# Second pair of a routed mixture-of-experts layer sorted by expert, first pair sorted one stage sooner

## What is computed

```
x = layernorm(h)
attn_out = softmax(q k^T / 4) v                      # 16 heads, all 512 keys, q k v = x W_qkv + b
gate = softmax(x W_gate + b_gate)                    # 8 experts
combine = the two largest gates of each token, zero for the other six experts
moe_out = sum over e of combine[e] * (x W_experts[e] + b_experts[e])
h = h + attn_out + moe_out
```

## Time and profile before

| what | us |
|---|---|
| median of 3 runs | 599.95 (599.64 to 600.82) |
| profiled execution, its span | 600.7 |
| TensorE busy | 539.3 (90%) |
| VectorE busy | 424.7 (71%) |
| ScalarE busy | 285.8 (48%) |
| GpSimd busy | 188.1 (31%) |
| stages 0 to 7, from each one's first score product | 51.0, 53.0, 53.1, 69.5, 60.7, 96.3, 85.2, 79.8 |

### The profile page before, as it was taken

How to read it: one execution, slowest core, us unless ns; L and a number is a source line. 1 busy time by engine, 2 the same in 40 slices (tenths; PEclk the granted TensorE clock), 3 DMA queues, 4 the chain that set the end, 5 groups by cost and what they waited for, 6 DMA issues and landing times.

```text
span 600.7 us, 9520 instructions
## 1 busy us (share of the span) xinstructions
PE 539.3 (90%) x3209; PEld 283.9 (47%) x3209; DVE 424.7 (71%) x941; ACT 285.8 (48%) x558; POOL 188.1 (31%) x257
## 2 busy tenths in 40 slices
PE   3968998989899899998888899989999999999996
PEld 2435554654565335334533456444545555544442
DVE  6757766667877895887678877656876566678841
ACT  0314454536544563676354343525565455444444
POOL 6444746223422600211243233202233331043201
PEclk9978999999999999999997899999999999999999
DMA  6364534222332343353235132403259667232311
GB/s 194 103 199 129 159 95 156 68 74 81 116 89 67 111 113 100 94 158 102 71 94 154 55 108 86 124 18 113 67 174 267 191 201 238 70 104 72 108 54 35
DMA packets 45151, 69.23 MB, mean 115 GB/s; under 512 B 9208, under 2 KB 38320, under 8 KB 42416
## 3 DMA queue, kind: packets, MB, share of 16 engines
q1 hardware_dynamic: 40672, 55.64, 31.5%
q0 software_dynamic: 4224, 12.59, 6.8%
q10 hardware_dynamic: 208, 0.40, 0.2%
HBM read 45.25 MB, written 23.07 MB: 114 GB/s over the span
## 4 chain that ended last, share of the span: by engine, by line
PE 67%; DVE 18%; issue 7%; DMA 3%; ACT 3%; POOL 1%; ACTq 0%; SPq 0%; DVEq 0%
PE OB L1593 12%; PE R L1473 10%; PE R L1368 9%; PE SC L1543 8%; PE ST L1566 7%; DVE neg_max L1048 5%; PE R L1383 4%; PE R L1459 4%; PE SC L1548 3%; PE ST L1572 2%; PE R L1419 2%; PE R L1487 2%; DVE neg_max L1056 2%; DMA QS<-shiftT 2%; PE SC L1553 2%
## 5 line engine op out<-in xcount | busy, mean ns | idle before, releaser
L1048 DVE TENSOR_REDUCE neg_max<-SC 128x1 f32<-128x512 f32 x256 | 170.8, 687 | 78.1 <-PE SC L1543 74.9
L909 ACT ACTIVATE prob<-ST 128x512 f32<-128x512 f32 x256 | 136.7, 598 | 123.9 <-PE ST L1566 118.7
L1593 PE MATMUL OB<-prob,VS 128*32 128x512 f32 (+2 forms) x1024 | 107.2, 491 | 0.1
L1543 PE MATMUL SC<-KS,QS 96*128 96x512 bf16 x256 | 97.6, 389 | 8.6 <-DVE neg_max L1048 6.6
L912 ACT ACTIVATE prob<-ST 128x512 f32<-128x512 f32 (+1 forms) x128 | 68.0, 543 | 68.2 <-PE ST L1572 67.9
L745 POOL TENSOR_SCALAR_AFFINE_SELECT prob<-prob 128x512 f32<-128x512 f32 x64 | 40.9, 639 | 131.1 <-ACT prob L912 131.0
L1566 PE MATMUL ST<-QS,KS 98*128 98x512 bf16 x256 | 77.5, 380 | 1.9 <-ACT prob L909 1.9
L1056 DVE TENSOR_REDUCE neg_max<-SC 128x2 f32<-128x512 f32 x64 | 44.1, 688 | 22.0 <-PE SC L1553 21.6
L1053 DVE TENSOR_REDUCE neg_max<-SC 128x1 f32<-128x128 f32 (+1 forms) x128 | 39.6, 351 | 25.8 <-PE SC L1553 25.5
L1548 PE MATMUL SC<-KS,QS 96*128 96x256 bf16 (+1 forms) x256 | 48.0, 270 | 6.2 <-DVE neg_max L1053 2.7
L1543 PEld LDWEIGHTS SC<-KS,QS 96*128 96x128 bf16 x256 | 24.8, 97 | 55.1 <-DVE neg_max L1048 35.9
(11 more groups left out here) (156 smaller groups left out, 765.1 us busy)
## 6 DMA issues: line engine op xcount, KB each, us to landing
scratch<-parts SPq DMA_DIRECT2D x96, 128.0 KB
QS<-scratch SPq DMA_DIRECT2D x42, 256.0 KB, 3.3
KS<-scratch SPq DMA_DIRECT2D x42, 256.0 KB, 3.9
x_sorted<-ys SPq DMA_DIRECT2D x24, 128.0 KB, 3.2
xs<-x_sorted SPq DMA_DIRECT2D x12, 256.0 KB
y_sorted<-ys SPq DMA_DIRECT2D x12, 256.0 KB
QS<-scratch SPq DMA_DIRECT2D x12, 128.0 KB, 2.6
w_exp<-in_L_ffn_W_experts SPq DMA_DIRECT2D x6, 256.0 KB, 3.3
```

The costliest lines, as they stand in the source:

```text
L909: act.activation(prob[:, u % 2, e, :], src[:, :], ACT.Exp, scale=SCALE).then_inc(s_prob, 1)
L1048: dve.tensor_reduce(own_max[:, i, head:head + 1], bank[:, :], AX.X, ALU.max, negate=True).then_inc(s_max, 1)
L1543: pe.matmul(bank[:, :], Q[0:SHIFT_ROW, head, i * P:(i + 1) * P], K[0:SHIFT_ROW, head, :], start=True, stop=True).then_inc(s_sc_ps, 1)
L1593: mm = pe.matmul(OB[VW * i:VW * (i + 1), columns], VS[s % 3][:, kt, v:v + VW], p_of, start=(kt == 0), stop=(kt == NT - 1), skip_group_chec ...
```

## The change

Batches 2 and 3 become a second sorted pair, and the dense path goes with its weight loads and its accumulations. Routing, scatters, loads, products, copies and stores exist once per pair (`r`), with rings counted through both. The first pair's routing moves to the end of stage 3, its products to stages 4 and 5, and `x_sorted` is zeroed in stage 2. The second pair is routed at the start of stage 6 and multiplied from its half slot 18 to half slot 10 of stage 7. Scatters and output gathers are issued two to a half slot instead of one, and tile `t` of a batch is added in step 3 + `t` instead of 6 + 2 `t`. Outputs are gathered in stage 5 (batch 0), 6 (batch 1) and 7 (batches 2 and 3). There is one `xT_full` instead of two, and the gathered outputs have four buffers instead of seven.

```diff
-    3: (("out", 2, 0), ("full", 1, 1)),
-    4: (("full", 2, 1), ("route", 0, 28), ("dense", 2, 32)),
-    5: (("route", 0, -4), ("dense", 2, 0), ("out", 3, 0), ("full", 3, 9), ("experts", 0, 36)),
-    6: (("full", 3, -23), ("experts", 0, 4), ("dense", 3, 29)),
-    7: (("experts", 0, -28), ("dense", 3, -3), ("combine", 0, 2), ("combine", 1, 10)),
+    3: (("out", 2, 0), ("full", 1, 1), ("route", 0, 24)),
+    4: (("full", 2, 1), ("route", 0, -8), ("experts", 0, 10)),
+    5: (("out", 3, 0), ("full", 3, 9), ("experts", 0, -22), ("combine", 0, 14)),
+    6: (("full", 3, -23), ("route", 1, 0), ("experts", 1, 18), ("combine", 1, 4)),
+    7: (("experts", 1, -14), ("combine", 2, 13), ("combine", 3, 17)),
...
+PAIR = 2
+PAIRS = B // PAIR
+PAIR_TILES = PAIR * NT
...
-LOAD_STEP, W_STEP, DENSE_W_STEP, STORE_STEP, ADD_STEP = -5, -3, -4, 4, 6
-
-EX_BEFORE = {2: 0, 0: DENSE_JOBS, 3: DENSE_JOBS + TILE_JOBS}
-W_BEFORE = {2: 0, 0: E, 3: E + EXPERT_TILES}
+LOAD_STEP, W_STEP, STORE_STEP, ADD_STEP = -5, -3, 4, 3
...
-        y = [buffer[:, k, :].rearrange("p (k d) -> p k d", k=TOP_K) for buffer in (xT_local, rest)
-             for k in (0, 1)] + xs
+        y = [xn_full[1][:, TOP_K * k:TOP_K * (k + 1), :] for k in (0, 1)] +\
+            [xT_local[:, k, :].rearrange("p (k d) -> p k d", k=TOP_K) for k in (0, 1)]
...
-            return xT_local if kind == LOCAL else xT_full[b % 2]
+            return xT_local if kind == LOCAL else xT_full
...
-            return xn_local if kind == LOCAL or b >= SPARSE else xn_full[b]
...
+            return xn_local if kind == LOCAL or b == 2 else xn_full[b % 3]
...
-            def load_sorted(i):
+            def load_sorted(r, i):
+                n = at(r, TILE_JOBS, i)
                 if i == 0:
-                    for b in range(SPARSE):
+                    for b in range(PAIR * r, PAIR * (r + 1)):
                         sp.wait_ge(s_sorted[b], 16 * NT * TOP_K)
...
-                    if s == 3 and u == 0:
+                    if s == 2 and u == 0:
                         sp.wait_ge(s_iota, 3)
-                    if s == 3 and u < EXPERT_TILES // 2:
+                    if s == 2 and u < EXPERT_TILES // 2:
                         zero_sorted(2 * u)
                         zero_sorted(2 * u + 1)
-                    for b, slot in ((2, 3), (0, 8), (1, 12)):
-                        if (s, u) == (LAST, slot):
+                    for b, stage, slot in ((0, 5, 15), (1, 6, 10), (2, 7, 13)):
+                        if (s, u) == (stage, slot):
                             write_out(b)
...
-            def sort_rows(n):
-
-                b, t, k = n // (NT * TOP_K), n // TOP_K % NT, n % TOP_K
+            def sort_rows(r, n):
+
+                b, t, k = PAIR * r + n // (NT * TOP_K), n // TOP_K % NT, n % TOP_K
                 if n == 0:
-                    pool.wait_ge(s_filled, 16 * EXPERT_TILES)
-                    pool.wait_ge(s_route, 8)
+                    pool.wait_ge(s_route, at(r, ROUTE_STEPS, 8))
+                    if r == 0:
+                        pool.wait_ge(s_filled, 16 * EXPERT_TILES)
+                    else:
+                        pool.wait_ge(s_xs_ps, at(r, TILE_JOBS, 0))
                 pool.indirect_dma_start(
                     x_sorted, bass.IndirectOffsetOnAxis(ap=slots[:, b * NT + t, k:k + 1].bitcast(U32), axis=0),
                     xn_of(STAGE[FULL, b])[:, t, :], None).then_inc(s_sorted[b], 16)
...
+                if n == 0:
+                    pool.wait_ge(s_qk_ps, at(STAGE[LOCAL, B - 1], 4, 4))
+                    pool.wait_ge(s_v_ps, V_BEFORE[STAGE[LOCAL, B - 1] + 1])
+                if n >= W_RING:
+                    pool.wait_ge(s_ex_ps, (n - W_RING) // 2 + 1)
...
             def gather_output(n, k):
+                r = n // PAIR_TILES
                 if n == 0 and k == 0:
-                    p = STAGE[FULL, B - 1]
                     pool.wait_ge(s_wo_ps, at(B - 1, 2, 2))
-                    pool.wait_ge(s_part2, at(p, 4, 4))
-                    pool.wait_ge(s_xs_ps, TILE_JOBS)
+                    pool.wait_ge(s_sorted[1], 16 * NT * TOP_K)
+                if n % PAIR_TILES == 0 and k == 0:
                     for j in range(Y_RING):
-                        pool.wait_ge(s_stored[j], ring_count(TILE_JOBS - Y_RING + j, Y_RING))
+                        pool.wait_ge(s_stored[j], ring_count(at(r, TILE_JOBS, TILE_JOBS) - Y_RING + j, Y_RING))
                 if n >= len(y) and k == 0:
-                    pool.wait_ge(s_moe, 2 * (n - len(y) + 1))
+                    pool.wait_ge(s_moe, TOP_K * (n - len(y) + 1))
                 pool.indirect_dma_start(
-                    y[n % len(y)][:, k, :], None, y_sorted,
+                    y[n % len(y)][:, k, :], None, y_sorted[r],
...
-                if b >= SPARSE:
-                    pool.wait_ge(s_dense, at(b - SPARSE, NT * E, NT * E))
+                if b == B - 1:
+                    pool.wait_ge(s_moe, at(b, TOP_K * NT, TOP_K * NT))
...
                 if what == "route":
                     for n in range(PAIR_TILES * TOP_K):
-                        if step == SCATTER_STEP + n:
-                            sort_rows(n)
+                        if step == SCATTER_STEP + n // 2:
...
                 if what == "combine":
                     for n in range(NT * TOP_K):
-                        if step == n:
+                        if step == n // TOP_K:
                             gather_output(b * NT + n // TOP_K, n % TOP_K)
...
-                if kind == FULL and b > 1:
-                    act.wait_ge(s_qk_ps, at(STAGE[FULL, b - 2], 4, 4))
-                    act.wait_ge(s_v_ps, V_BEFORE[STAGE[FULL, b - 2] + 1])
+                if kind == FULL and b > 0:
+                    act.wait_ge(s_qk_ps, at(STAGE[FULL, b - 1], 4, 4))
+                    act.wait_ge(s_v_ps, V_BEFORE[STAGE[FULL, b - 1] + 1])
...
                     dve.wait_ge(s_rstd, p + 1)
                     if p > 0:
                         dve.wait_ge(s_x_ps, at(p, NC, 0))
+                    if kind == FULL and b == B - 1:
+                        dve.wait_ge(s_sorted[0], 16 * NT * TOP_K)
...
-                if quarter == 4 and b < SPARSE:
-                    tiles = slice(b * NT, (b + 1) * NT)
+                if quarter == 4:
+                    tiles = slice(b % PAIR * NT, (b % PAIR + 1) * NT)
...
             def add_outputs(b, t):
 
                 n = b * NT + t
-                dve.wait_ge(s_yadd, at(b, G, G))
+                if b < B - 1:
+                    dve.wait_ge(s_yadd, at(b, G, G))
                 dve.wait_ge(s_yb, at(b, 2, 2))
                 dve.wait_ge(s_y[n % len(y)], 2 * ring_count(n, len(y)))
...
                 if what == "combine":
                     for t in range(NT):
-                        if step == ADD_STEP + TOP_K * t:
+                        if step == ADD_STEP + t:
                             add_outputs(b, t)
```

More of the change, by code:

```diff
@@ L234, in prep_jobs @@
                  if step == first + 2 * i]
-    if what == "dense":
-        jobs += [("dx", b, i) for i in range(DENSE_JOBS) if step == 2 * i]
     return jobs
@@ L363, in tower @@
         tile_row = sb("tile_row", [P, EXPERT_TILES])
-        w_rows = sb("w_rows", [P, EXPERT_TILES], I32)
+        w_rows = [sb(f"w_rows{r}", [P, EXPERT_TILES], I32) for r in range(PAIRS)]
         SC = [ctx.enter_context(nc.psum_tensor(f"SC{i}", [P, T], F32)) for i in (0, 1)]
@@ L559, in prep @@
                         if step == LOAD_STEP + 2 * i:
-                            load_sorted(i)
+                            load_sorted(b, i)
                         if step == STORE_STEP + 2 * i:
-                            store_outputs(i)
-                if what == "dense":
-                    for e in range(E):
-                        if step == DENSE_W_STEP + 4 * e:
-                            load_weights(b, e)
+                            store_outputs(b, i)
             def stack_biases():
@@ L1177, in tile_experts @@
+                route_step(r, dve.tensor_copy(slots[:, r * PAIR_TILES:(r + 1) * PAIR_TILES, :], slot_f[:, :, :]), 8)
+            def tile_experts(r):
+                route_step(r, dve.tensor_tensor(ends[:, :], base[:, :], blocks[:, :], ALU.add), 9)
+                route_step(r, dve.tensor_tensor(
                     ended[:, :, :], ends[:, :].unsqueeze(1).to_broadcast([P, EXPERT_TILES, E]),
                     tile_no[:, :].unsqueeze(2).to_broadcast([P, EXPERT_TILES, E]), ALU.is_le), 10)
-                route_step(dve.tensor_reduce(tile_expert[:, :], ended[:, :, :], AX.X, ALU.add), 11)
@@ L1421, in project_out, with count_rows @@
                 mm.then_inc(s_wo_ps, 1)
[L1423 to L1426 removed]
+            def count_rows(r):
+                bank = claim(("route", r, 0))
                 pe.wait_ge(s_no, 5)
[L1428 removed]
+                pe.wait_ge(s_sel, PAIR * (r + 1))
                 cols = bank[:, 0:(PAIR_TILES + 1) * E].rearrange("p (t e) -> p t e", e=E)
@@ L1436, in count_rows, with turn_sorted @@
```

(16 more changed lines are left out.)

203 lines of the change are left out of this document (72 added, 131 removed).

## The result

The changed kernel takes **622.85 us** (median, 617.80 to 627.71) where the kernel before takes 600.38 beside it: a ratio of 1.0331, 95% interval 1.0273 to 1.0388. It is slower, as forecast to be the likelier side, but by 22.5 us where 4 were forecast, and above the range of 584 to 614.

The account below looks back on a forecast made before the run. It took TensorE, busy 90% of the span, as the bound, with jobs paid in full in stages 5 to 7. Terms -26.5 + 3.5 + 3.3 + 7 + 12 + 4.5 + 0 + 0.5 = +4.3 gave 604 us, range 584 to 614.

Parts of the forecast that it names:

- the side: Whole kernel: slower was the likeliest outcome, chance 0.51, against 0.36 for faster and 0.13 for the same.
- Loss 13.5, less half a slot of lead: +12: Stage 6: batch 1's gathers share GpSimd with the second pair's scatters, so VectorE waits; +12 us, bounds 6 and 16.
- Stage 4 gains ten jobs and eleven transposes: 17.3 + 5.2 = +22.5: Stage 4, TensorE: added sorted jobs and transposes cost +22.5 us, with +18 as low end if idle time is filled.
- +7 for the scatters: Start of stage 4: the first pair's scatters on GpSimd delay masks and the reciprocal deviation; +7 us, bounds 2 and 10.
- the clock at 0: TensorE clock: -3 us for filling a thin stretch of stage 4, +3 behind new waits; net 0, -3 to +6.
- routing: One VectorE chain moves from stage 4 to 3, a second enters stage 6; net +3.3 us, 1 to 4.5.
- the eight adds lie beside products, at nothing; without that cover, 3.8: Stage 5, VectorE: eight output adds are hidden beside products and cost nothing; uncovered, 3.8 us.
- the last output is stored at about 33.5 us and lands by 36.7: Stage 7: times into the stage after which sixteen gathers start; part of a +4.5 us term, 0 to 7.
- the last six slots of 2.46 hide that: End of stage 7: batch 3's last tile, added near 60.5 us, is hidden by six slots of 2.46 us.
- The waits mostly vanish: Faster rival, stages 4, 6 and 7: 580.7 us without three waits, 592 with half of each; chance 0.28.
- The queues cost more: Slower rival: scatters land later than gathers, loads come late in stage 6, clock stays halved through waits; 613 us, chance 0.17.
- The products' bounds (-20 to -31): TensorE work over stages 4 to 7, dense jobs removed and sorted jobs added: sum -26.5 us, with these bounds.

Follow-up runs that it names:

- that with everything: Changed kernel with first pair's products later, its scatters one per half slot, its adds in stages 6 and 7, second pair's scatters, stores, gathers sooner: 587.27 us.
- filler: Changed kernel with each pair of local score products in slots 1 to 4 of stage 4 issued six times instead of once: 621.59 us, 1.0339.

## Why the prediction was right and wrong

**Right: the side, and stage 6.** "Loss 13.5, less half a slot of lead: +12" measured 12.5 us of waiting (10.9 to 12.5 in three other runs with this stage 6), and 8.3 to 11.9 us came back when it was taken away. Queue position times 1.26 us plus landing, against the moment at which VectorE asks, was the right method; these eight gathers landed in 4.2 us (median), near the 3.9 of the earlier trace rows.

**Wrong: "Stage 4 gains ten jobs and eleven transposes: 17.3 + 5.2 = +22.5", with +18 as the low end.** This is the step that failed most: slots 5 to 15 took 28.6 us more, where 22.5 less 3.3 of routing and 3 of clock are 16.2. The durations came from stages in which a job stands alone between scores, and were bounded only downwards, by idle time to be filled. In slots 5 to 8 jobs share two banks with batch 2's projections and cost 14.7 us instead of 7.1; begun behind the projections, the same jobs gave some 5 us back. A warning was to be had: a sorted job is two dependent parts with a copy on ScalarE between, and slots 5 to 8 already took 18.8 us, 4.7 each.

**Wrong: "from slot 14 of stage 3, which now starts at 272.39", and so "5.7 us in all", +7 for the scatters.** They cost 11.7 us. The pace held: 1.26 us each without a gap, twelve ahead of the reciprocal deviation. What failed is the start. An attention add stands ahead of the first scatter in GpSimd's queue and waits for VectorE; the trace of the kernel before has it behind 272.39 already:

```profile
273.99 0.73 POOL L786 TENSOR_TENSOR h<-h,AO 128x256 f32<-128x256 f32 x1 [10.01 <-DVE AO L1090]
```

Counted from the start of stage 4, the first scatter was forecast 6.3 us ahead of it and came 2.2 ahead; so the deviation was done at 15.3 us instead of 11.4, the third mask at 21.7 instead of 18.0, and 9.8 us were lost by then instead of 5.7. The other 1.9 are work at half clock behind that mask; with them the term passed its upper bound of 10.

**Wrong: the clock at 0.** It counted -3 in stage 4 for filling the stretch of the earlier trace rows, and +3 behind the waits. The stage's clock stayed at 0.90 (0.92 before). Half clock cost 1.9 us in its slot 4, 2.0 in stage 2 and 1.7 in stage 5 of the profiled run; what it cost in stages 6 and 7 was not taken apart. Its weight shows between executions of one kernel: that with everything took 582.53 us at a mean granted clock of 0.986 and 590.88 at 0.966.

**Wrong places, small sum: routing.** Stage 3 was to lose 3.3 us and lost none (but VectorE's `AO` for GpSimd's add came 1.6 us later in the stage), stage 4 was to gain 3.3; its slots 9 to 15 took 13.9 us more, where 15.4 of jobs less 3.3 and 3 make 9.1. What of these 4.8 is routing and what clock was not separated.

**Stage 5: "the eight adds lie beside products, at nothing; without that cover, 3.8".** They cost 1.8, by the last tile's alone. With the 1.7 of clock that leaves 1.5 of the 5.0, for which no run was made.

**Stage 7: "the last output is stored at about 33.5 us and lands by 36.7".** The copy was done in time (579.4, 31.4 us in), but the store stood behind shift rows on SyncE, a queue that the forecast had not walked there. And "the last six slots of 2.46 hide that" did not hold: the last slot took 11.2 us where it was 8.8.

**The rivals.** "The waits mostly vanish" was decided where it said: the first add of batch 1 found its tile at 478.6, 21 us into stage 6, not by 17. "The queues cost more" had a late landing as its mechanism; scatters landed in 2.4 us, earlier than the gathers, so its 613 was nearer for another reason; its clock at half through the waits did come, in 17.1 us of stage 4. The Trainium skill ("DMA: Bandwidth & Descriptors", "Anatomy of one DMA — SWDGE (gpsimd) path") gave an estimate of 2.3 us for such a transfer: the scatters agree (2.4), the gathers don't (3.3). The 1 us between them decides little, as what came late was the issue. The median time to landing in the page's list of issues:

```profile
x_sorted<-xn_full,slots POOLq DMA_INDIRECT x24, 2.4
...
xn_full<-y_sorted,slots POOLq DMA_INDIRECT x16, 3.3
```

The range was too narrow. The products' bounds (-20 to -31) left 6.5 us above their estimate, and stage 4's alone came 12.4 above theirs. The resolution of 0.2% was too fine as well: the intervals here reach 0.3 to 0.9% to either side.

## What to carry to other kernels

Price a moved job with the durations of the place it goes to: between projections that share its banks, jobs that come to 7.1 us alone cost 14.7. When a table gives an in-order engine two slow issues where it had one, walk everything behind them in that queue, each on top of the last, from the moment at which the instruction ahead of them lets the first one start. Walk SyncE's queue too: here pace, place and order alone, with no work removed, turned 3.3% slower into 1.7% faster.

## What the chip showed that was not expected

The granted clock was half in 17.1 us of stage 4's start. Up to the third mask this cost nothing: with the clock whole for most of that time (filler) the masks came at the same points of the stage. Behind that mask it cost 1.9 us. The row of that stretch in the changed kernel:

```profile
286.30:303.40 17.10, 11.83 (x59) 6.84 (x52) 3.82 (x10) 3.13 (x6) 14.32 (x18) 0.50 0.35 108
```

TensorE looks 69% busy there, 11.83 of 17.10 us, and still GpSimd's queue set the time up to 299.4: busy time at half clock is no sign of a bound. The scatter of 128 rows landed in 2.4 us, the gather of as many in 3.3 (4.2 among the eight of stage 6), while both hold GpSimd for the same 1.26.
